# Shift products on four 32-row tiles, issued ahead of the scores, in an attention and spike kernel on one core

## What is computed

```python
xn = layernorm(x)
q, k, v = heads(xn @ w_qkv)                  # 16 heads of 16
q, k = spectral_filter(q), spectral_filter(k)
attn = softmax(q @ k.T / 4)                  # 2048 x 2048 for each of 2 x 16 heads
y = relu(xn @ W_fc.T) ** 2 @ W_proj.T
spikes = five steps of mem = 0.9 mem + y - reset, counted where mem > 1
out = x + (attn @ v) @ w_out + b_out + spikes / 5
```

## Time and profile before

| | |
|---|---|
| Median of 3 runs | 1691.33 us (1690.95 to 1692.08) |
| Span of the profiled execution, first to last instruction | 1689.3 us |
| Busy PE / PEld | 1681.4 / 1145.9 us |
| Busy DVE / ACT / POOL | 1494.2 / 1330.1 / 719.7 us |
| DMA, share of 16 engines | about 0.2 in the long middle stretch |

### The profile page before, as it was taken

How to read it: one execution, slowest core, us unless ns; L and a number is a source line. 1 busy time by engine, 2 the same in 40 slices (tenths; PEclk the granted TensorE clock), 3 DMA queues, 4 the chain that set the end, 5 groups by cost and what they waited for, 6 DMA issues and landing times.

```text
span 1689.3 us, 44435 instructions
## 1 busy us (share of the span) xinstructions
PE 1681.4 (100%) x17842; PEld 1145.9 (68%) x17842; DVE 1494.2 (88%) x2375; ACT 1330.1 (79%) x1718; POOL 719.7 (43%) x979
## 2 busy tenths in 40 slices
PE   9999999999999999999999999999999999999999
PEld 6566666666666666666666666666666666666667
DVE  6889999998999999989998999999989998999884
ACT  5548888888888888888888888888888888888872
POOL 3103334555433345554333455543335554333455
PEclk9999999999999999999999999999999999999999
DMA  6851122112211221122112211221122112211133
GB/s 216 294 161 47 33 54 55 51 33 55 55 50 34 55 55 43 41 55 55 43 41 55 56 37 47 55 55 36 48 55 56 31 53 55 55 30 54 43 105 103
DMA packets 95406, 108.02 MB, mean 64 GB/s; under 512 B 56032, under 2 KB 70240, under 8 KB 95200
## 3 DMA queue, kind: packets, MB, share of 16 engines
q1 hardware_dynamic: 91744, 101.97, 21.2%
q10 hardware_dynamic: 3456, 3.21, 0.6%
HBM read 78.91 MB, written 20.97 MB: 59 GB/s over the span
## 4 chain that ended last, share of the span: by engine, by line
PE 98%; DVE 1%; ACT 0%; issue 0%; ACTq 0%; POOL 0%; POOLq 0%
PE banks L735 31%; PE ring L711 22%; PE ring L718 14%; PE ring L724 14%; PE banks L841 7%; PE banks L846 3%; PE banks L659 2%; PE ring L928 2%; PE ring L672 1%; PE ring L645 1%; PE ring L659 1%; PE ring L686 0%; DVE stats L947 0%; DVE attnT L979 0%; ACT xnT L513 0%
## 5 line engine op out<-in xcount | busy, mean ns | idle before, releaser
L562 ACT ACTIVATE probs<-ring 128x1024 f32<-128x1024 f32 x1024 | 1002.1, 1026 | 6.5 <-PE ring L724 6.2
L711 PE MATMUL ring<-kst,qst 64*128 64x512 f32 x2000 | 674.7, 417 | 0.3 <-ACT probs L562 0.3
L735 PE MATMUL banks<-probs,vst 128*32 128x256 f32 x8192 | 548.2, 385 | 0.1
L1036 DVE TENSOR_REDUCE pmax<-ring 128x2 f32<-128x1024 f32 x407 | 497.7, 1223 | 12.7 <-PE ring L711 0.5
L568 ACT ACTIVATE half_sb<-ring 128x512 f32<-128x512 f32 x500 | 299.2, 598 | 261.4 <-PE ring L711 254.1
L718 PE MATMUL ring<-qst,kst 64*128 64x512 f32 x2048 | 493.0, 425 | 0.1
L711 PEld LDWEIGHTS ring<-kst,qst 64*128 64x128 f32 x2000 | 328.3, 184 | 208.3 <-issue 204.6
L1017 DVE TENSOR_REDUCE pmax<-ring 128x1 f32<-128x512 f32 x500 | 345.4, 691 | 88.7 <-PE ring L711 85.1
L724 PE MATMUL ring<-shift_rows,ones 64*128 64x512 f32 x2048 | 422.9, 390 | 0.0
L1023 DVE TENSOR_REDUCE pmax<-half_sb 128x1 f32<-128x512 f32 x500 | 335.5, 671 | 37.0 <-ACT half_sb L568 33.1
L735 PEld LDWEIGHTS banks<-probs,vst 128*32 128x32 f32 x8192 | 213.7, 109 | 209.7 <-issue 91.0
(11 more groups left out here) (96 smaller groups left out, 1050.9 us busy)
## 6 DMA issues: line engine op xcount, KB each, us to landing
kst<-qk_scratch SPq DMA_DIRECT2D x256, 128.0 KB, 3.0
qst<-qk_scratch SPq DMA_DIRECT2D x256, 128.0 KB, 2.9
qk_scratch<-attnT SPq DMA_DIRECT2D x32, 256.0 KB, 3.0
shift_rows<-shiftT SPq DMA_DIRECT2D x512, 2.0 KB
qk_scratch<-probs SPq DMA_DIRECT2D x16, 256.0 KB, 3.0
attnT<-o_turned SPq DMA_DIRECT2D x256, 16.0 KB, 1.9
xnT<-x SPq DMA_DIRECT2D x8, 512.0 KB, 5.6
out<-xnT SPq DMA_DIRECT2D x7, 512.0 KB, 2.9
```

The source lines that it names most:

```text
L562: act.activation(probs[:, s % PS, :], score_slot(g), ACT.Exp, scale=SCALE).then_inc(exp_done, 1)
L711: return pe.matmul(unit_slot(g)[:, c * BLK:(c + 1) * BLK], qst[b][rows, tile * P:(tile + 1) * P], kst[b][rows, key:key + BLK], start=True, ...
L735: mm = pe.matmul(po[32 * j:32 * (j + 1), half * D:(half + 1) * D], vst[b][:, kt, :], quarters[:, j], start=(kt == 0), stop=(kt == TB - 1))
L1036: dve.tensor_reduce(pmax[:, tile, 2 * part:2 * part + 2], unit_slot(g).rearrange("p (c e) -> p c e", c=2), AX, ALU.max).then_inc(mx_taken, 1)
```

## The change

`store_shift` writes the two rows of the shift to partitions 0, 32, 64 and 96 instead of 0 and 64, four DMAs for each. `shifted` works on one of four groups of 32 rows, starts the accumulation group in place of ending it and carries no semaphore; `scores` ends it and signals `score_ready`. In the usual branch of `pair` the four shift products of both steps come first, on four different groups and in four different PSUM banks, behind the waits for both slots; the four score products follow. In the branch of the last head the order is written anew. The setting of all of `shift_rows` to zero and of `ones` to one is as before.

```diff
-SHIFT = 8 * 16
+SHIFT = 16 * 16
+GROUPS = 4
+GROUP = P // GROUPS
@@ store_shift
-                for side in range(2):
-                    dst = shift_rows[side * SIDE:side * SIDE + 2, cols].rearrange("r (t j q) -> r t j q", j=4, q=32)
+                for group in range(GROUPS):
+                    dst = shift_rows[group * GROUP:group * GROUP + 2, cols].rearrange("r (t j q) -> r t j q", j=4, q=32)
                     for j in range(4):
                         sp.dma_start(dst[:, :, j, :].bitcast(F32), shiftT[32 * j:32 * j + 16, :]).then_inc(shift_in, 16)
@@ scores, shifted
-                pe.matmul(score_slot(g)[:, c * BLK:(c + 1) * BLK], kst[b][rows_of(side), kt * P:(kt + 1) * P],
-                          qst[b][rows_of(side), q:q + BLK], start=True, stop=False)
-
-            def shifted(g, s, side, c):
-
-                q = s // TB * HALF + c * BLK
-                mm = pe.matmul(score_slot(g)[:, c * BLK:(c + 1) * BLK], ones[rows_of(side), :],
-                               shift_rows[rows_of(side), q:q + BLK], start=False, stop=True)
+                mm = pe.matmul(score_slot(g)[:, c * BLK:(c + 1) * BLK], kst[b][rows_of(side), kt * P:(kt + 1) * P],
+                               qst[b][rows_of(side), q:q + BLK], start=False, stop=True)
                 if c == 1:
                     mm.then_inc(score_ready, 1)
+
+            def shifted(g, s, group, c):
+
+                q, rows = s // TB * HALF + c * BLK, slice(group * GROUP, (group + 1) * GROUP)
+                pe.matmul(score_slot(g)[:, c * BLK:(c + 1) * BLK], ones[rows, :],
+                          shift_rows[rows, q:q + BLK], start=True, stop=False)
@@ pair, the usual branch
-                    scores(g, even, sb_, 0, 0)
                     if late_copy(g):
                         pe.wait_ge(mx_taken, taken(g - 1))
+                    score_free(g + 1)
+                    shifted(g, even, 0, 0)
+                    shifted(g, even, 2, 1)
+                    shifted(g + 1, odd, 1, 0)
+                    shifted(g + 1, odd, 3, 1)
+                    scores(g, even, sb_, 0, 0)
                     scores(g, even, sb_, 1, 1)
-                    shifted(g, even, 0, 0)
-                    shifted(g, even, 1, 1)
-                    score_free(g + 1)
                     scores(g + 1, odd, sb_, 0, 0)
                     scores(g + 1, odd, sb_, 1, 1)
-                    shifted(g + 1, odd, 0, 0)
-                    shifted(g + 1, odd, 1, 1)
@@ pair, the branch of the last head
                 elif scored:
+                    shifted(g, even, 0, 0)
+                    share(1, 0)
+                    shifted(g, even, 1, 1)
+                    share(1, 1)
                     scores(g, even, sb_, 0, 0)
-                    share(1, 0)
+                    score_free(g + 1)
+                    shifted(g + 1, odd, 2, 0)
                     scores(g, even, sb_, 0, 1)
-                    share(1, 1)
-                    shifted(g, even, 0, 0)
-                    score_free(g + 1)
+                    shifted(g + 1, odd, 3, 1)
+                    share(0, 0)
                     scores(g + 1, odd, sb_, 1, 0)
-                    shifted(g, even, 0, 1)
+                    share(0, 1)
                     scores(g + 1, odd, sb_, 1, 1)
-                    share(0, 0)
-                    shifted(g + 1, odd, 1, 0)
-                    share(0, 1)
-                    shifted(g + 1, odd, 1, 1)
```

## The result

The changed kernel takes 2131.01 us (median of 4 runs, 2128.55 to 2135.05) where the kernel before takes 1691.7: a ratio of 1.260, 95% interval 1.258 to 1.262. The forecast was 2064, the range 1930 to 2160, 0.97 for slower. The profiled execution has a span of 2133.2 us, 443.9 more than before.

A forecast was written before the change was run, and what follows sets the result against it. PE, busy for the whole span, was taken to bound the kernel. 1689.3 + 91 (pairs) + 211 (stalls) + 19 (last head) = 2010, + 52 (clock) + 2.0 (span to median) = 2064 us; range 1930 to 2160.

The forecast's parts named there:

- The bound: Whole kernel: PE is busy throughout and 98% of the last chain, so PE time added to a pair lengthens the end.
- Two changes of rows a pair: Ordinary pairs: two more tile-row changes at 0.20 us, one 0.23 us wave saved; pair 3.21 us, +91 us over 503.
- The late shift: SP's queue: sixteen issues land the shift 13.7 us after its pair starts; PE stalls 3.4 us, 62 times, 211 us.
- Waiting for both slots before the first shift product costs nothing.: Ordinary pair: ScalarE's exponentials end early enough that awaiting both slots adds nothing in a 3.21 us pair.
- The clock: PE idle in stalls: the granted clock falls behind two of five, 25 x 2.1 = 52 us, bounds 0 and 186.
- rival (b): Stalls: the clock falls in every one, 62 x 2.1 to 3.0 us, total 2142 to 2198 us; chance 0.17.
- The last head: Nine pairs of the last head: seven changes at 0.20 and 0.7 for waves, +2.1 us each, 19 us.
- (a): Pairs: 32 and 64 rows mix without emptying the array, pair 2.81 us; total 1871 to 2001, middle 1960; chance 0.20.
- (d): Whole kernel faster: shift reaches all groups in time, rows mix freely, 1573 us; needs about 0.33 us an issue; chance 0.02.

The follow-up runs named there:

- the kernel with four changes: Changed kernel with eight issues, the two steps' shift products apart again on 32-row tiles (shift, scores, shift, scores): 2153.64 us, ratio 1.274.
- the late wait: Changed kernel's order on 64-row tiles with eight issues, odd step's wait and shift products put back behind the even step's scores: 1695.31 us, ratio 1.0019.
- the kernel with eight issues: Changed kernel with eight DMA issues of 32 partitions for sixteen, rows of two neighbouring groups side by side: 1858.92 us, ratio 1.098.
- The repaired order: Changed kernel with the last head's nine pairs reordered: four shift products first, the other eight products in twos behind them: 2090.0 us.

## Why the prediction was right, and where not

**The bound.** Right: PE set the pair, and everything added to it came out at the end. 2131 lies in the range, 67 us above the forecast; most of that is the last head (31 us) and the clock behind the stalls (21 us).

**Two changes of rows a pair.** Right, to the hundredth: 3.21 us for a pair, 0.20 a change. It had been read from a change between 128 and 64 rows. The Trainium skill (TensorEngine Tiling (Array Packing), Key Properties) says that a change of tiling mode drains TensorE. The trace agrees for a change between 32 and 64 rows: a group of one wave took 0.43 us for 0.23, and again in each group of the kernel with four changes.

**The late shift.** Right: 62 stalls of 3.36 us, 208.6 in all, for 62 of 3.4, 211. Sixteen issues at 10.5 us and 13.59 us from the pair's start to the load were both worked out from eight issues of the kernel before. The landing, for which no row of before stood, came out at 13.59 - 2.00 - 15 x 0.66 = 1.7 us, the value chosen between 1.0 and 2.7.

**"Waiting for both slots before the first shift product costs nothing."** Wrong. I took the ordinary pair, where ScalarE is done 0.15 us into the next, for all pairs, and did not look at the three of each head behind an extra copy, for which the kernel before swaps its slots. In the changed kernel little of it shows: of the three, s = 10 and 26 come between the first DMA and the stall, so the stall hides them. With 64-row tiles the early waits cost 60 us, the late wait gives 56 of them back.

**The clock.** The direction was right, both numbers off, in opposite ways: 25 losses at 2.1 us = 52 us forecast, 58 at 1.25 = 73 measured, so part of the agreement is luck. The count is nearly rival (b)'s; its price (2.1 and more) was too high, and so its 2142 to 2198 too. The price came from the first products of the kernel before. Only their longer records spoke for the lower level there: the window over them stands at 1.00.
```profile
0.00:6.40 6.40, 5.32 (x13) 4.24 (x14) 2.38 (x13) 2.77 (x3) 3.36 (x11) 1.00 0.62 178
```
A stretch behind a stall of 3.36 us was cheaper, one behind 4.15 us cost 2.3.

**The last head.** The mis-sized term: 19 us forecast, 9 x 2.1. It measured some 50 (nine pairs in 73.6 us for 23.3). I had the changes and the lost company of the products, 2.56 + 2.1 = 4.7 us a pair, and in the kernel with eight issues the first of the nine, still at the full clock, lasts 4.64. What I put at nothing is the clock in these pairs: it falls to half and stays there for 71.7 us, and the last eight pairs take 8.49 us each. The repaired order keeps it up but for the stretch behind the last half's stall. What in the old order brings it down, the changes or the products left without company, was not separated.

**Two slips in the rivals.** In (a) the shift products would start 0.65 - 0.10 = 0.55 us into their pair by the prediction's own figures, not 0.45, which makes it 6 us less. In (d) 116 us over 62 halves are 1.9 us of stall, or 0.12 for each of fifteen issues, so the change turns into none near 0.46 us an issue and not 0.4. At 0.66 neither moves the verdict.

Added up: 91 for the pairs, 209 for the stalls, 73 for the clock behind them and 50 for the last head are 423 of the 439 us. The 16 that are left were not taken apart.

## What to carry to other kernels

A product that seems to use little of the array is not free to shrink: if its neighbours stay on other tile sizes, each change costs the array running empty and one uncovered load of weights, here 0.20 us against 0.23 for the wave saved. Count DMA issues as well as bytes: eight more issues of 2 KB, 0.66 us each on one queue, cost more (272 us) than what was done to the matmuls (167, the kernel with eight issues), since the completion before was only some 2.73 - 1.7 = 1.0 us ahead of its user. And before a wait is moved forward, look at the pairs in which its releaser is late, not at the ordinary one.

## What the runs showed of the hardware that I had not expected

- The granted clock can fall after the idle time is over. With stalls of 4.15 us it fell 1.5 to 2.0 us ahead of their end, for 62 of 63, at 2.3 us of cost for each; with 3.36 us from 0.3 us ahead of the end to 1.9 behind it, for 58 of 62, at 1.25; with 2.2 us 1.1 to 1.8 us behind it, for 24 of 62; with 0.9 us for none.
- Products of no use in a stall paid: 75 us less time for 1736 products more (62 x 28).
- Busy records don't keep the clock up: in the last head PE is busy for 69.00 of 69.00 us and the clock is at 0.50.
- DMAs of 32 partitions are issued nearly as fast as those of 16 (0.63 us for 0.61): with eight of them for sixteen no wait was left.
